# Starting addresses of the expert layers' split activations in SBUF, 16 and 48 bytes past a multiple of 256

## The chip, the cores and the metric

The kernel runs on one core of a Trainium2 chip. The metric is the device time of one launch in microseconds (us), as the median of several runs. Three runs of the kernel before gave 1542.0, 1543.3 and 1543.79 us. Engines are named as in the profile: PE is TensorE (its weight loads are shown apart as PEld), DVE is VectorE, ACT is ScalarE, POOL is GpSimd, SP is SyncE, which issues the DMAs.

## What is computed

One transformer layer on x of shape [16, 512, 128] in float32: a state-space mixer with residual and layer norm, then a mixture of 12 experts with residual and layer norm. Only the second half touches the change. Cut to that:

```python
dw1, dw2, dw3 = (top3_softmax(x_addr @ U.T) for U in (U1, U2, U3))   # [tokens, 12]
h = sum over e of dw1[:, e] * (x @ W1[e].T)      # [tokens, 512]
h = gelu(h)
y = sum over e of dw2[:, e] * (h @ W2[e].T)      # [tokens, 128]
y = y + dw3 @ b2
```

All 12 experts are computed densely for every token. The mixer also has one product of this kind that matters here, `silu(z) @ Wzg`.

## The kernel before, in words

The 16 sequences are 16 batches of 512 tokens. The program is one long straight list of instructions for each engine, written out by hand in Python: `body` is called once for each batch and lays, between the mixer steps of batch b, the expert steps of batch b-1, so that PE always has an expert product to work on while other engines prepare mixer operands. Semaphores order the engines; there is no scheduler, and SBUF tensors are placed one behind the other in the order in which `sb(...)` names them, each start rounded up to 32 bytes.

Large products are made in a split form. A float32 value is written as a high half (rounded to the type fp32r) and a low half (the rest, also fp32r), and `mm3` (lines 240 to 250) multiplies with three matmuls, each over 512 moving columns: high by high (L247), high by low (L248), low by high (L249):

```python
nc.tensor.matmul(ps, s_hi, m_hi, ...)         # L247: stationary s_hi, moving m_hi
nc.tensor.matmul(ps, s_hi, m_lo, ...)         # L248
last = nc.tensor.matmul(ps, s_lo, m_hi, ...)  # L249
```

Every one of these loads its own stationary operand of 128 columns first (a LDWEIGHTS on PEld). A row of the profile names the moving operand first and the stationary one second: `exp_bank<-sp_hi,w_hi` has `sp_hi` moving.

The split activations live in two tensors, `sp_hi` and `sp_lo`, each [128, 4, 512] in fp32r (line 144), so 8192 bytes in each partition. They are used in three places:

- `expert_in` (first expert layer): for each expert and each of 4 hidden slices of 128, one `mm3` with the weights `w1_hi`, `w1_lo` stationary and one quarter of `sp_hi`, `sp_lo` moving. 48 times three matmuls in a batch, except that expert 0 of the last batch reads `xT_hi`, `xT_lo`.
- `expert_out` (second expert layer): for each of 4 token blocks, 3 column groups and 4 slices, one `mm3` with a 128-column block of `sp_hi`, `sp_lo` stationary and `w2_hi`, `w2_lo` moving. 48 times three in a batch.
- `mix_zg`: 8 times three in a batch, `wzg_hi`, `wzg_lo` stationary and `sp_hi`, `sp_lo` moving.

They are written by casts on ACT (L1186, L641) or DVE (L1236) for the high half, and by a subtraction on POOL (L1190, L644, L1242) or DVE (L1239) for the low half, each of 128 partitions by 512 elements in most cases.

Line 103 puts an otherwise unused tensor `before_lines` of 128 bytes ahead of the weights. With it, the tensors `w1_hi` to `w2_lo`, `wbc`, `wz`, `wx`, `wzg`, `xT_hi`, `xT_lo`, `fbuf`, `acc` and also `sp_hi` (byte 209920) and `sp_lo` (byte 218112) all start at a multiple of 256 bytes, and so does every slice of them that a matmul of 512 columns reads. After `sp_lo` come only small tensors (`ix`, `ssum`, `dw2`, `dwpad`, `nrm`, `delta`, `a_rows`, `a_hi`, `a_lo`, `wbdt`, `router` and others), whose starts lie anywhere in steps of 32 bytes: `router` at 32 past a multiple of 256, `a_hi` at 96, `a_lo` and `a_rows` at 224, `dwpad` at 128.

Of the kernel before, what the change touches and what calls it, by code (L numbers as in the profile page):

```python
# [8 lines left out]
F32R = mybir.dt.float32r  # L9
# [6 lines left out]
P = 128  # L16
D = 128
NB, T = 16, 512
# [8 lines left out]
NH = HID // P  # L27
# [58 lines left out]
def layer_program(nc, x, Wz, Win, Wzg, Wout, dt_bias, A_log, D_param, P_w, U1T, U2T, U3T, W1T, W2T, b2, out):  # L86
    ctx = ExitStack()
    with ctx:
        def sb(name, shape, dt=F32):
            return ctx.enter_context(nc.sbuf_tensor(name, shape, dt))  # L90
# [50 lines left out]
        acc = sb("acc", [P, NC, D])  # L141
        acc_odd = sb("acc_odd", [P, D])
        wide = [fbuf[:, 2, :], fbuf[:, 3, :]]
        sp_hi, sp_lo = sb("sp_hi", [P, NH, T], F32R), sb("sp_lo", [P, NH, T], F32R)
        lg = fbuf[:, 3, 0:NC * NR * E].rearrange("p (g e) -> p g e", e=E)
        mx = fbuf[:, 3, NC * NR * E:NC * NR * (E + 8)].rearrange("p (g e) -> p g e", e=8)
        ix = sb("ix", [P, NC * NR, 8], U32)
# [1655 lines left out]
```

How the kernel before makes its waits and increments, by code:

```python
        def wait(eng, name, b, k=None):  # L213
            p = prods[name]
            v = (b.off - p.start) * p.n * p.step + ((p.n if k is None else k) - p.less) * p.step
            seen = waited.setdefault(id(eng), {})
            if (b.reg is None and v <= 0) or seen.get(name, -10**9) >= v:
                return
            seen[name] = v
            eng.wait_ge(p.sem, v if b.reg is None else b.reg * (p.n * p.step) + v)
            if eng is SP:
                alone(SP)
# [75 lines left out]
        def round_rest(n, src, hi, lo):  # L299
            DVE.tensor_copy(hi, src).then_inc(sems["chain"], 1)
            DVE.wait_ge(sems["chain"], n)
            DVE.tensor_tensor(lo, src, hi.bitcast(F32), ALU.subtract).then_inc(sems["cast"], 1)
# [1 line left out]
        def setup(eng):  # L305
# [3 lines left out]
                SP.dma_start(st_wz, Wz[:, :]).then_inc(sems["wz"], 16)  # L309
                SP.dma_start(bias_b[:, :], dt_bias.partition_broadcast(P)).then_inc(sems["decay_par"], 16)
                SP.dma_start(neg_a[:, :], A_log.partition_broadcast(P)).then_inc(sems["decay_par"], 16)
                SP.dma_start(d_b[:, :], D_param.partition_broadcast(P)).then_inc(sems["decay_par"], 16)
                SP.dma_start(st_wzg, Wzg.rearrange("(k p) n -> p k n", p=P)).then_inc(sems["wzg"], 16)
                SP.wait_ge(sems["pad"], 5)
                SP.dma_start(dA_dram.rearrange("h (c t) -> (h c) t", t=P), cum_t[0:H * NC, :]).then_inc(sems["zero"], 16)
                SP.dma_start(pw, P_w[:, :]).then_inc(sems["small"], 16)
```

## Time and profile before

| what | value |
|---|---|
| median of three runs | 1543.3 us (1542.0 to 1543.79) |
| the profiled execution's own time | 1542.65 us |
| its span, first to last instruction | 1540.9 us |
| mean granted TensorE clock | 0.998 of full speed |
| PE busy | 1525.7 us, 99% of the span, 8646 matmuls |
| DVE, ACT, POOL busy | 1115.0, 598.1, 658.3 us |
| DMA | 73 GB/s over the span |

The busy time of an engine is the time in which at least one of its instructions was under way. Matmuls overlap: the next one starts before the one ahead has ended, so the mean duration of a matmul (some 390 ns) is not what it costs. What it costs is the distance from its start to the next one's start, which is read from the timeline. The chain of waits tells which engine's work the end of the program follows from.

### The profile page before, as it was taken

How to read it: one execution, taken by the hardware profiler on the slowest of the kernel's cores; microseconds unless marked ns; L12 is line 12 of the kernel's file. 1: busy time of each engine (PE TensorE's matmuls, PEld its weight loads, DVE VectorE, ACT ScalarE, POOL GpSimd, SP SyncE). 2: the span in 40 equal slices, each digit the busy share in tenths (PEclk: the TensorE clock that was granted, in tenths of full speed). 3: DMA queues.
4: the chain of work that ended last, by engine and by line, in shares of the span. 5: the costliest groups of instructions: out<-in, count | busy, mean ns of one | idle time of the engine just before them, and what ended most of it. 6: DMA issues, size and time to landing. Idle time of an engine off the chain costs nothing.

```text
span 1540.9 us, 25335 instructions
## 1 busy us (share of the span) xinstructions
PE 1525.7 (99%) x8646; PEld 1250.4 (81%) x8646; DVE 1115.0 (72%) x3113; ACT 598.1 (39%) x1360; POOL 658.3 (43%) x751
## 2 busy tenths in 40 slices
PE   9999999999999999999999999999999999999998
PEld 7778888888888888888788888888888888887886
DVE  7677776877768687686776768777686776767755
ACT  6643424425244351533525244242443515335130
POOL 6671623616145270643616336162451705436040
PEclk9999999999999999999999999999999999999999
DMA  6340312314023140321403123040230403214020
GB/s 180 100 148 29 118 42 67 100 29 135 18 77 90 30 137 15 103 71 46 120 11 125 45 61 106 28 132 21 72 95 29 138 15 96 76 39 128 14 78 7
DMA packets 81456, 114.53 MB, mean 74 GB/s; under 512 B 10144, under 2 KB 37296, under 8 KB 81328
## 3 DMA queue, kind: packets, MB, share of 16 engines
q1 hardware_dynamic: 81328, 112.92, 24.6%
q8 instruction: 68, 1.11, 0.3%
q14 instruction: 60, 0.49, 0.1%
HBM read 107.76 MB, written 5.13 MB: 73 GB/s over the span
## 4 chain that ended last, share of the span: by engine, by line
PE 93%; POOL 3%; DVE 1%; issue 1%; DMA 1%; SPq 0%; ACT 0%; POOLq 0%; DVEq 0%
PE exp_bank L247 23%; PE exp_bank L249 22%; PE exp_bank L248 22%; PE mix_bank L896 4%; PE mix_bank L922 3%; PE mix_bank L247 3%; PE mix_bank L249 3%; PE mix_bank L904 3%; PE mix_bank L248 3%; PE mix_bank L793 1%; PE turn_bank L1249 1%; PE mix_bank L525 1%; PE mix_bank L739 1%; PE mix_bank L1013 1%; POOL Wt L856 1%
## 5 line engine op out<-in xcount | busy, mean ns | idle before, releaser
L1190 POOL TENSOR_TENSOR sp_lo<-fbuf,sp_hi 128x512 fp32r<-128x512 f32 (+2 forms) x201 | 243.4, 1214 | 176.9 <-ACT sp_hi L1186 106.9
L247 PE MATMUL exp_bank<-w_hi,sp_hi 128*128 128x512 f32 x768 | 304.0, 396 | 0.8 <-POOL sp_lo L1242 0.8
L247 PE MATMUL exp_bank<-sp_hi,w_hi 128*128 128x512 f32 x764 | 303.5, 397 | 0.1
L249 PE MATMUL exp_bank<-w_hi,sp_lo 128*128 128x512 f32 x768 | 299.7, 390 | 0.0
L248 PE MATMUL exp_bank<-w_lo,sp_hi 128*128 128x512 f32 x768 | 298.9, 389 | 0.0
L249 PE MATMUL exp_bank<-sp_hi,w_lo 128*128 128x512 f32 x764 | 298.3, 391 | 0.0
L248 PE MATMUL exp_bank<-sp_lo,w_hi 128*128 128x512 f32 x764 | 297.8, 390 | 0.0
L1289 DVE SCALAR_TENSOR_TENSOR acc<-exp_bank,dw,acc 128x128 f32<-128x128 f32 x384 | 132.4, 345 | 137.2 <-PE exp_bank L249 136.6
L1186 ACT CAST sp_hi<-fbuf 128x512 fp32r<-128x512 f32 (+2 forms) x203 | 120.0, 592 | 272.5 <-DVE fbuf L1156 216.5
L856 POOL TENSOR_TENSOR Wt<-Wt,Gh 128x512 f32<-128x512 f32 x128 | 184.8, 1445 | 21.0 <-DVE Wt L848 21.0
L247 PEld LDWEIGHTS exp_bank<-sp_hi,w_hi 128*128 128x128 f32 x764 | 143.7, 188 | 38.2 <-issue 8.9
L559 POOL TENSOR_TENSOR delta<-delta,bias_b 128x32 f32<-128x32 f32 x16 | 4.1, 256 | 388.4 <-ACT delta L535 383.7
L249 PEld LDWEIGHTS exp_bank<-w_hi,sp_lo 128*128 128x128 f32 x768 | 144.1, 188 | 31.1
L247 PEld LDWEIGHTS exp_bank<-w_hi,sp_hi 128*128 128x128 f32 x768 | 144.2, 188 | 30.8 <-POOL sp_lo L1242 1.3
L822 ACT ACTIVATE Gh<-Gm,delta 128x128 f32<-128x128 f32 x512 | 163.7, 391 | 13.2 <-POOL Wt L856 13.2
L249 PEld LDWEIGHTS exp_bank<-sp_hi,w_lo 128*128 128x128 f32 x764 | 143.7, 188 | 31.0
L248 PEld LDWEIGHTS exp_bank<-w_lo,sp_hi 128*128 128x128 f32 x768 | 144.4, 188 | 28.8
L248 PEld LDWEIGHTS exp_bank<-sp_lo,w_hi 128*128 128x128 f32 x764 | 143.8, 188 | 28.7
L848 DVE TENSOR_TENSOR_SCAN Wt<-seg_b,unit_bank 128x512 f32<-128x512 f32 x124 | 149.5, 1207 | 22.7 <-PE mix_bank L904 19.7
L1156 DVE TENSOR_TENSOR fbuf<-turn_bank,row_b 128x512 f32<-128x512 f32 x189 | 126.8, 675 | 11.4 <-DMA row_b<-dw_rows 11.1
L1289 DVE SCALAR_TENSOR_TENSOR acc_odd<-exp_bank,dw,acc_odd 128x128 f32<-128x128 f32 x320 | 109.4, 342 | 0.0
L1242 POOL TENSOR_TENSOR sp_lo<-fbuf,sp_hi 128x512 fp32r<-128x512 f32 x30 | 40.0, 1332 | 135.2 <-DVE sp_hi L1236 135.2
(267 smaller groups left out, 2286.1 us busy)
## 6 DMA issues: line engine op xcount, KB each, us to landing
row_b<-dw_rows SPq DMA_DIRECT2D x189, 256.0 KB, 3.3
seg_b<-dA_rows SPq DMA_DIRECT2D x124, 256.0 KB, 3.5
ctd<-cum_rows SPq DMA_DIRECT2D x128, 96.0 KB, 3.2
x_in<-in_x SPq DMA_DIRECT2D x16, 256.0 KB, 2.8
result<-acc SPq DMA_DIRECT2D x15, 256.0 KB, 2.2
fbuf<-in_W1T SPq DMA_DIRECT2D x12, 256.0 KB, 3.5
acc<-in_W2T SPq DMA_DIRECT2D x5, 256.0 KB, 3.5
x_in<-in_W2T SPq DMA_DIRECT2D x5, 256.0 KB, 2.8
```

Source lines behind the costliest of these rows:

```text
L247: nc.tensor.matmul(ps, s_hi, m_hi, start=start and j == 0, stop=False, skip_group_check=onto)
L248: nc.tensor.matmul(ps, s_hi, m_lo, start=False, stop=False, skip_group_check=onto)
L249: last = nc.tensor.matmul(ps, s_lo, m_hi, start=False, stop=stop and j == n - 1, skip_group_check=onto)
L822: last = AC.activation(G[:, c, :], Gm[:, c, :], ACT.Copy, scale=delta[:, c, h:h + 1])
L848: sig("scan", DVE.tensor_tensor_scan(W, first_seg[h % 4] if first(b) else seg_b[h % 2][:, :], unit[:, :], 0.0, ALU.mult, ALU.add))
L856: sig("W", PO.tensor_tensor(W, W, Gh[h % 2][:, :, :].rearrange("p c t -> p (c t)"), ALU.mult))
L896: PE.matmul(ps[j * HD:(j + 1) * HD, tok(c)], Xd[:, c, h * HD:(h + 1) * HD], Wt[:, q % 2, at:at + P], start=(c == 0 and not first(b)), stop ...
L904: last = PE.matmul(ps[j * HD:(j + 1) * HD, tok(c)], S[n, c - 1, q * HD:(q + 1) * HD], ctd[n, q % 2, (c - 1) * P:c * P], start=False, stop= ...
L1156: sig("xw", DVE.tensor_tensor(wide[e % 2], rb[:, :], row_b[e % 2][:, :], ALU.mult))
L1186: sig("xw_hi", AC.copy(hi[:, cols], wide[e % 2][:, cols]))
L1190: sig("xw_lo", on.tensor_tensor(lo[:, cols], wide[e % 2][:, cols], hi[:, cols].bitcast(F32), ALU.subtract))
L1289: sig("comb", DVE.scalar_tensor_tensor(dst, ps, w, dst, ALU.mult, ALU.add))
```

## The change

The two tensors of split activations get 16 bytes of padding at either end, and the program uses the part between. Nothing else is edited; each engine has the same instructions in the same order, with the same shapes and waits.

```diff
-        sp_hi, sp_lo = sb("sp_hi", [P, NH, T], F32R), sb("sp_lo", [P, NH, T], F32R)
+        LINE = 4
+        sp_hi, sp_lo = (sb(n, [P, NH * T + 2 * LINE], F32R)[:, LINE:LINE + NH * T].rearrange("p (k t) -> p k t", k=NH)
+                        for n in ("sp_hi", "sp_lo"))
```

The padded `sp_hi` is 8224 bytes long and still begins at byte 209920, so its used part begins at 209936, 16 past a multiple of 256. The padded `sp_lo` begins at 218144 and its used part at 218160, 48 past a multiple of 256. A quarter of either is 2048 bytes and a block of 128 columns is 512 bytes, so every slice that a matmul, a cast or a subtraction touches has the same 16 or 48. The small tensors behind them all move up by 64 bytes, so `router` is now 96 past a multiple of 256, `a_hi` 160, `a_rows` and `a_lo` 32 and `dwpad` 192. Lines behind the edit have numbers that are higher by 2.

## Rows read from the trace of the kernel before

**Rows 1.** The page: busy time, the granted clock in 40 slices, the chain that ended last
```profile
PE 1525.7 (99%) x8646; PEld 1250.4 (81%) x8646; DVE 1115.0 (72%) x3113; ACT 598.1 (39%) x1360; POOL 658.3 (43%) x751
...
PEclk9999999999999999999999999999999999999999
...
PE 93%; POOL 3%; DVE 1%; issue 1%; DMA 1%; SPq 0%; ACT 0%; POOLq 0%; DVEq 0%
```
**Rows 2.** Waits of PE over the whole span: us in total, times, longest
```profile
PE mix_bank L896 <- POOL Wt L856: 2.4, 1, 2.4
PE turn_bank L1464 <- POOL ident L325: 2.2, 1, 2.2
PE exp_bank L247 <- POOL sp_lo L1242: 0.8, 1, 0.8
```
**Rows 3.** Busy time in two batches of the steady part, with matmul counts and clock
```profile
core 0: us, PE busy (x) PEld busy (x) DVE busy (x) ACT busy (x) POOL busy (x), PEclk, DMA share, GB/s
585.68:679.43 93.75, 93.75 (x531) 76.91 (x531) 68.70 (x195) 36.22 (x83) 39.60 (x45) 1.00 0.24 72
679.43:773.16 93.73, 93.73 (x531) 76.91 (x531) 68.71 (x195) 36.20 (x83) 39.58 (x45) 1.00 0.24 71
```
**Rows 4.** Groups of matmuls on sp_hi and sp_lo: xcount, busy us, mean ns
```profile
L249 PE MATMUL exp_bank<-w_hi,sp_lo 128*128 128x512 f32 x768 | 299.7, 390 | 0.0
L248 PE MATMUL exp_bank<-sp_lo,w_hi 128*128 128x512 f32 x764 | 297.8, 390 | 0.0
L247 PE MATMUL mix_bank<-sp_hi,wzg_hi 128*128 128x512 f32 x120 | 46.8, 390 | 0.2 <-ACT fbuf L1080 0.2
L247 PE MATMUL exp_bank<-sp_hi,wzg_hi 128*128 128x512 f32 x8 | 3.2, 401 | 0.0
```
**Rows 5.** Timeline of PE, steady stretch of 512-column matmuls: start us, us, instruction
```profile
632.03 0.39 PE L249 MATMUL exp_bank<-sp_hi,w_lo 128*128 128x512 f32 x1
632.25 0.39 PE L247 MATMUL mix_bank<-wx_hi,xT_hi 128*128 128x512 f32 x1
...
641.55 0.39 PE L249 MATMUL exp_bank<-sp_hi,w_lo 128*128 128x512 f32 x1
```
**Rows 6.** The same timeline just ahead, behind short matmuls
```profile
628.93 0.27 PE L678 MATMUL mix_bank<-ident,a_rows 128*32 128x128 f32 x1
628.96 0.26 PE L752 MATMUL mix_bank<-a_hi,strict_r 128*128 128x24 f32 x1
629.07 0.26 PE L752 MATMUL mix_bank<-a_lo,strict_r 128*128 128x24 f32 x1
629.18 0.39 PE L754 MATMUL mix_bank<-a_rows,upper 128*128 128x32 f32 x2
629.40 0.47 PE L247 MATMUL exp_bank<-sp_hi,w_hi 128*128 128x512 f32 x1
629.72 0.39 PE L248 MATMUL exp_bank<-sp_lo,w_hi 128*128 128x512 f32 x1
629.95 0.40 PE L249 MATMUL exp_bank<-sp_hi,w_lo 128*128 128x512 f32 x1
630.18 0.40 PE L247 MATMUL exp_bank<-sp_hi,w_hi 128*128 128x512 f32 x1
630.42 0.39 PE L248 MATMUL exp_bank<-sp_lo,w_hi 128*128 128x512 f32 x1
630.64 0.39 PE L249 MATMUL exp_bank<-sp_hi,w_lo 128*128 128x512 f32 x1
```
**Rows 7.** The chain of waits in order of time: a stretch of 32 short matmuls
```profile
679.43 3.58 PE mix_bank L922 x32
```
**Rows 8.** Durations of the instructions that write the split halves, min/median/max
```profile
L1186 ACT CAST sp_hi<-fbuf x203: 297/621/627, 74.2 to 1489.2; 128x512 fp32r<-128x512 f32 x88, 128x384 fp32r<-128x384 f32 x7, 128x128 fp32r<-128x128 f32 x7
L1190 POOL TENSOR_TENSOR sp_lo<-fbuf,sp_hi x201: 456/1291/1593, 79.5 to 1490.2; 128x512 fp32r<-128x512 f32 x87, 128x384 fp32r<-128x384 f32 x7, 128x128 fp32r<-128x128 f32 x7
L1242 POOL TENSOR_TENSOR sp_lo<-zg,sp_hi x2: 1282/1332/1383, 1499.2 to 1501.9; 128x512 fp32r<-128x512 f32 x2
```

## Prediction

> **What bounds the kernel now.** I read the page first. PE is busy for 1525.7 of 1540.9 us, every slice shows a full granted clock (2.4 GHz), and the chain that ended last is 93% PE [rows 1]. Then the waits of PE: the longest entry is 2.4 us, once, and the only one on a tensor of this change is 0.8 us, once, on `sp_lo` in the last batch [rows 2]. Then two batches of the steady part side by side: both take 93.7 us, PE is busy for all of it with 531 matmuls, and the two agree to 0.02 us [rows 3]. So for the time only one thing counts: how far apart PE's matmuls start. What ACT, DVE and POOL do is hidden, until one of them makes PE wait.
>
> The distance of starts is read from the timeline. From the matmul at 632.03 to the one at 641.55 there are 42 steps in 9.52 us, or **226.7 ns a step** [rows 5]. That stretch holds matmuls with `sp_hi` or `sp_lo` moving and others with `wx` and `xT` only, and all step alike. 512 columns at 2.4 GHz are 213.3 ns, so each step has 13.4 ns on top, while the next 128 stationary columns are read from SBUF beside the 512 moving ones. Every operand in that stretch starts at a multiple of 256 bytes. Behind short matmuls the pace is worse for a while: from 629.72 to 632.03 there are ten steps in 2.31 us, 231.0 ns each, with 0.22 us as the shortest (630.42 to 630.64) and 0.47 us for two as the longest (629.95 to 630.42) [rows 5, 6]. So the step isn't a constant of 512 columns; something of a few nanoseconds in it varies, then settles.
>
> **How many matmuls the change reaches.** With `sp_hi` or `sp_lo` as an operand: three groups of 768 in the second expert layer, three of 764 in the first, three of 120 + 8 in `mix_zg` (one row of each kind stands in [rows 4]). Together 2304 + 2292 + 384 = 4980. At 226.7 ns they fill 1129 us of the span. One nanosecond a step is worth 4.98 us, and what a measurement of this kernel can tell from no change, 0.2% or 3.1 us, is 0.62 ns a step.
>
> **The change, part by part.**
>
> 1. *Reads of the moving operand from 16 or 48 instead of 0* (first layer and `mix_zg`, 2676 matmuls). The trace has no 512-column matmul off a multiple of 256. The nearest rows are short ones: moving `a_hi` (96 past), `a_lo` and `a_rows` (224 past) start 0.11 us apart [rows 6], as do the 32 short ones on aligned `wout` and `zg`, 3.58 / 32 = 0.112 us [rows 7]. So an odd start costs nothing that two digits show, but these read 24 to 32 columns and are paced by the load of 128 stationary columns, so the cover would hide a few nanoseconds. Price taken: 0.
> 2. *Loads of the stationary operand from 16 or 48* (second layer, 2304). The weight load runs beside the matmul ahead, and PEld is busy for 76.91 of 93.75 us [rows 3], so a load that was one column longer stays hidden. Price taken: 0.
> 3. *The two reads against each other.* This is what can't be excluded. Bounds from both sides: at best the whole 13.4 ns go, 4980 x 13.4 = 67 us, so 1543 - 67 = 1476; at worst each step is like the slowest pair, 235 ns, 4980 x 8.3 = +41 us, so 1584. The steady row is the nearest to both ends, because it shows steps untouched by all else that reads and writes SBUF meanwhile: DVE busy 68.70, POOL 39.60 and DMA a quarter of the time in a batch, and still one pace [rows 3, 5]. A read path that let those streams pass unfelt is not likely to care which 16 bytes an operand starts with. Price taken: 0.
> 4. *Writes of the halves to 16 and 48* by ACT, POOL and DVE. The medians are 621 and 1291 ns [rows 8]. If each became a tenth longer (0.06 and 0.13 us), PE, which waits for `sp_lo` once in the program [rows 2], would feel it at that one place, below 0.3 us with both subtractions of the last batch [rows 8]. Cover: every half is made well ahead of its product. Price 0 to +0.3 us.
> 5. *The small tensors moved by 64 bytes.* Moves of 64 keep their starts at odd places, where they were already. Price 0.
>
> The sum: 0 + 0 + 0 + 0.3 at most. The profiled execution took 1542.65 us (its span and 1.75 around it), 0.65 below the median of the runs. I forecast the median unchanged, **1543.3 us**.
>
> **A rule on each side.** Steps off a multiple of 256 but on a multiple of 16 are seen at 0.11 us like the others [rows 6, 7]. By that rule, the trace agrees: the Trainium skill, SBUF — State Buffer, Specifications (TRN2), says that SBUF is read in lines of 16 bytes, and 16 and 48 both keep every operand on a line, by which the sum is 0. Against that stands the 226.7 ns, which the same skill would not give: TensorE: Matmul & The Clock Gate, section "Wait — 56ns, not 53.3ns?", has N columns at 2.4 GHz plus about 2.5 ns, which I work out as an estimate of 215.8 ns for 512. No row here shows that pace.
>
> **The rivals.**
>
> *A. No change* (1540 to 1546): as above.
>
> *B. Faster: the stationary and the moving stream collide because both start at the same place in SBUF.* For it: 13.4 ns that the columns don't explain are paid at each step; a load of 128 columns is 32 pieces of 16 bytes, and 13.4 ns are 32 cycles at 2.4 GHz, one for each piece; and the settling behind short matmuls looks like two streams finding a phase. Shifting one of them by an odd number of 16-byte pieces would end it. Against it: the moving stream passes about two columns (512 in 213.3 ns) for each one of the load (128 in at most 112 ns, the step of short matmuls that each load 128 [rows 7]), so their relation sweeps through all phases within one matmul whatever the start. Prices: if steps go to the shortest one seen, 0.22 us, 4980 x 6.7 = 33 us, 1510; if five sixths of the 13.4 go, 55 us, 1488; all of it 1476. A step with nothing on top is seen nowhere in this trace, so I leave the last sixth out.
>
> *C. Slower: the pace doesn't settle, or an operand that starts inside a larger block costs one more fetch.* Place: all 4980. If they step as behind short matmuls, 231.0 ns, that is 4980 x 4.3 = +21 us, **1565**; one extra cycle at 1.2 GHz (0.83 ns) would be +4 us, 1547. It decides from 0.62 ns a step. For it: all operands of the steady 226.7 are aligned, and nothing shows that they need not be; the ten slower steps show that this path can run slower for more than 2 us. Against it: the short matmuls off alignment. At the slowest pair's pace it would be 1584.
>
> *D. Slower through an engine off PE*: writes at odd starts grow so much that PE waits. It takes more than the idle time ahead of those engines; POOL is busy 39.60 of 93.75 us [rows 3]. Below 1546 if at all.
>
> **How the numbers follow.** A 0.42 (with D's harmless part); B 0.30, of it 0.14 near 1510 and 0.16 near or below 1488; C 0.26, of it 0.19 up to 1566 and 0.07 beyond; D 0.02. Hence faster 0.30, same 0.42, slower 0.28. The likeliest case has a range of its own of 1540 to 1546. Since cases of both signs hold most of the chance, the range reaches to five sixths of the excess below (1488) and to the unsettled pace above (1566), and leaves out some 0.1 to 0.15: the last part of B and the worst of C.
>
> **What the changed profile would show.** A: 42 steps in 9.52 us in the stretch behind `mix_ends`, 93.7 us a batch. B or C: the steps of matmuls on `sp_hi`/`sp_lo` away from 226.7 ns, while those in the same stretch with `wx` and `xT` alone, which the change doesn't touch, stay at it; a steady batch has 144 + 144 + 24 = 312 steps of the first kind, so its 93.7 us move by 0.31 us for each nanosecond. If the two layers differ, it is the moving or the stationary read alone. D: new rows in PE's waits on `sp_hi` or `sp_lo`. The prediction is wrong if the batch moves by more than 0.2 us.

## The result, and the profile after

The changed kernel takes 1563.03 us (median of four runs, 1561.27 to 1563.69); the kernel before, on the same chip, 1542.78 us. The ratio is 1.0128 with a 95% interval from 1.0116 to 1.014: **slower by 20 us**. The forecast was no change; the time lies in the stated range, two us below what rival C gave (1565).

The page of the changed kernel, lines that answer to [rows 1]:

```profile
PE 1545.3 (99%) x8646; PEld 1252.5 (80%) x8646; DVE 1110.8 (71%) x3113; ACT 598.2 (38%) x1360; POOL 658.5 (42%) x751
...
PEclk9999999999999999999999999999999999999999
...
PE 92%; POOL 3%; DVE 1%; issue 1%; DMA 1%; SPq 0%; ACT 0%; POOLq 0%; DVEq 0%; ACTq 0%
```

The span grew from 1540.9 to 1561.2 us, and PE's busy time by 19.6 us with it, at the same granted clock. ACT and POOL are busy as long as before. The waits of PE, against [rows 2]:

```profile
PE turn_bank L1466 <- POOL ident L327: 2.2, 1, 2.2
PE mix_bank L898 <- POOL Wt L858: 2.2, 1, 2.2
PE exp_bank L249 <- POOL sp_lo L1244: 0.8, 1, 0.8
```

No wait has grown. Busy time in two batches of the steady part, against [rows 3]:

```profile
core 0: us, PE busy (x) PEld busy (x) DVE busy (x) ACT busy (x) POOL busy (x), PEclk, DMA share, GB/s
592.53:687.54 95.01, 95.01 (x532) 77.09 (x531) 68.60 (x195) 36.20 (x83) 39.67 (x45) 1.00 0.24 71
687.54:782.56 95.02, 95.02 (x532) 77.09 (x531) 68.58 (x195) 36.20 (x83) 39.61 (x45) 1.00 0.25 70
```

A batch takes 95.02 us where it took 93.74, 1.28 more, and 16 batches of that are 20.5 us, against 20.3 by which the span grew: the whole loss. The same matmuls simply start farther apart. The timeline of PE in the stretch of [rows 5] (start us, us, instruction):

```profile
639.64 0.39 PE L251 MATMUL exp_bank<-sp_hi,w_lo 128*128 128x512 f32 x1
639.87 0.40 PE L249 MATMUL mix_bank<-wx_hi,xT_hi 128*128 128x512 f32 x1
640.10 0.40 PE L250 MATMUL mix_bank<-wx_lo,xT_hi 128*128 128x512 f32 x1
640.34 0.40 PE L251 MATMUL mix_bank<-wx_hi,xT_lo 128*128 128x512 f32 x1
640.57 0.39 PE L249 MATMUL mix_bank<-sp_hi,wzg_hi 128*128 128x512 f32 x1
...
649.35 0.39 PE L251 MATMUL exp_bank<-sp_hi,w_lo 128*128 128x512 f32 x1
```

The same 42 steps take 9.71 us instead of 9.52: 231.2 ns a step instead of 226.7. The three matmuls on `wx` and `xT`, whose operands stand where they stood, take 0.70 us (639.87 to 640.57), so they too step more than 230 ns each. In the second expert layer it is slower still:

```profile
608.71 0.39 PE L251 MATMUL exp_bank<-w_hi,sp_lo 128*128 128x512 f32 x1
...
610.81 0.39 PE L251 MATMUL exp_bank<-w_hi,sp_lo 128*128 128x512 f32 x1
...
612.91 0.40 PE L251 MATMUL exp_bank<-w_hi,sp_lo 128*128 128x512 f32 x1
```

18 steps in 4.20 us are 233.3 ns each, in the settled part of a stretch, and each half of them takes 2.10 us. In the kernel before, the pace of 231 ns lasted for ten steps behind short matmuls [rows 6] and then fell to 226.7. Now a stretch of the second layer stays at 233.3, and one of the first at 230 to 231.

These are settled paces too, only slower ones. The trace holds the starts to the nanosecond, finer than the views print them. In the kernel before, the steps of a settled stretch are 226, 227, 227, over and over. In the changed kernel those of the second layer are 236, 233, 231, over and over: an unbroken stretch of 36 matmuls of that layer ends at 226.7 ns a step in all 45 cases before, and at 233.3 in all 45 cases after.

### The profile page after: what moved, and what is told of

The parts are those of the page before. It is cut to its first block, busy times and chain, and to the rows that moved or that the text cites. A ratio compares the mean times of both kernels' runs of the same rounds, so it can differ in the third digit from the quotient of the medians.

```text
span 1561.2 us, 25335 instructions
## 1 busy us (share of the span) xinstructions
PE 1545.3 (99%) x8646; PEld 1252.5 (80%) x8646; DVE 1110.8 (71%) x3113; ACT 598.2 (38%) x1360; POOL 658.5 (42%) x751
## 4 chain that ended last, share of the span: by engine, by line
PE 92%; POOL 3%; DVE 1%; issue 1%; DMA 1%; SPq 0%; ACT 0%; POOLq 0%; DVEq 0%; ACTq 0%
PE exp_bank L249 23%; PE exp_bank L250 22%; PE exp_bank L251 22%; PE mix_bank L898 4%; PE mix_bank L924 3%; PE mix_bank L249 3%; PE mix_bank L251 3%; PE mix_bank L250 3%; PE mix_bank L906 3%; PE mix_bank L795 1%; PE turn_bank L1251 1%; POOL w_lo L447 1%; PE mix_bank L741 1%; PE mix_bank L1015 1%; PE mix_bank L527 1%
## 5 line engine op out<-in xcount | busy, mean ns | idle before, releaser
L249 PE MATMUL exp_bank<-w_hi,sp_hi 128*128 128x512 f32 x768 | 308.1, 401 | 0.8 <-POOL sp_lo L1244 0.8
L250 PE MATMUL exp_bank<-w_lo,sp_hi 128*128 128x512 f32 x768 | 304.3, 396 | 0.0
```

Of the source, the lines that this page charges most:

```text
L249: nc.tensor.matmul(ps, s_hi, m_hi, start=start and j == 0, stop=False, skip_group_check=onto)
L250: nc.tensor.matmul(ps, s_hi, m_lo, start=False, stop=False, skip_group_check=onto)
```

## The experiments

All are edits of the kernel before. A time of one execution is given; where runs were repeated, the median and the interval. The kernel before gave 1542.0 to 1544.4 us beside them. The finest measure is the length of a batch, read from the chain of waits as the distance between two neighbouring stretches of 32 matmuls on `wout` and `zg`; in the kernel before it is 93.7 us [rows 3, 7]. "Place" is the start modulo 256 bytes.

**Which part of the change, and how far.** Four kernels. `small64` leaves the halves alone and moves the small tensors:

```diff
         sp_hi, sp_lo = sb("sp_hi", [P, NH, T], F32R), sb("sp_lo", [P, NH, T], F32R)
+        sb("behind", [P, 16])
```

> The two split halves stay at multiples of 256; only the small tensors behind them move up by 64 bytes, as in the change. Theory of the two streams (the step of a 512-column matmul depends on how far the start of the moving operand and the start of the stationary operand lie apart in SBUF, modulo some small power of two) and theory of the block (an operand that starts inside a larger block costs one more fetch): both expect no change, 93.74 us a batch and about 1543 us, since the large operands don't move. Theory of the small tensors (a read or write of one of them at its new place is slow): 95.0 us a batch and 1563 us.

`both16`, `both32` and `both64` put both halves into one tensor of 16448 bytes that starts at a multiple of 256, at the place n (4, 8 or 16 elements), with the small tensors moved as in the change:

```diff
-        sp_hi, sp_lo = sb("sp_hi", [P, NH, T], F32R), sb("sp_lo", [P, NH, T], F32R)
+        halves = sb("sp_halves", [P, 4112], F32R)
+        sp_hi = halves[:, n:n + NH * T].rearrange("p (k t) -> p k t", k=NH)
+        sp_lo = halves[:, NH * T + n:n + 2 * NH * T].rearrange("p (k t) -> p k t", k=NH)
```

> Both halves at 16 past a multiple of 64, weights at multiples, small tensors as in the change. Two streams: slower as the change, since moving and stationary start 16 bytes apart, 94.5 to 95.2 us a batch and 1555 to 1566 us. Block larger than 16 bytes: the same 95.0 us a batch. A third theory, that the difference between high and low half (32 bytes) is what costs, as the moving operand changes from one to the other within each group of three: no change, 93.74 us.

> Both halves at 32 past a multiple of 64. Two streams: if the period is 32 bytes, 93.74 us a batch; if it is 64 or more, another pace than 226.7 ns, either way, 93 to 95.5 us a batch. Block: 93.74 us if the block is 32 bytes, 95.0 us (1563) if it is 64 or more.

> Both halves at 64 past a multiple of 256. Two streams: no change if the period is 64 bytes or less (93.74 us a batch, 1543 us). Block: no change for a block of 64 bytes or less, 95.0 us a batch for one of 128 or 256.

Measured: `small64` 1542.98 us; `both16` 1559.62; `both32` 1569.4; `both64` 1562.89. The chain of `small64` and of `both32`:

```profile
585.49 3.58 PE mix_bank L923 x32
679.25 3.58 PE mix_bank L923 x32
```

```profile
593.90 3.58 PE mix_bank L924 x32
689.40 3.58 PE mix_bank L924 x32
```

93.76 and 95.50 us a batch. The small tensors cost nothing. A difference between high and low half isn't needed (`both16` has none). Any block or period of 64 bytes or less is ruled out by `both64`.

**One place for all, or a certain place?** `all32` makes the unused tensor ahead of the weights 160 bytes long, `all128` leaves it out, and `halves128` leaves it out and puts the halves back to a multiple of 256:

```diff
-        sb("before_lines", [P, 32])
+        sb("before_lines", [P, 40])      # all32; in all128 and halves128 the line is left out
```

> Every SBUF tensor, weights and halves alike, starts 32 bytes higher than in the kernel before, so nothing is at a multiple of 256 but moving and stationary operands keep their distance of 0. Theory of the relation (the step depends on how far the two operands that are read at once lie apart): no change, 93.74 us a batch, 1543 us. Theory of the absolute place (a start at other than 0 modulo 256 costs by itself): as with both halves at 32 or more, 95.5 us a batch and 1569 us.

> The unused 128 bytes ahead of the weights are left out, so all large tensors start 128 past a multiple of 256, with distance 0 between the two operands. Relation: 1543 us. Absolute place: slower, unless its period is 128 bytes or less; but halves at 64 were slow, so it would be 128 at least.

> Weights and the mixer's operands at 128 past a multiple of 256, halves at a multiple of 256: distance 128. Relation with a period of 128 bytes: 1543 us, 93.74 us a batch. Relation with a period of 256 or more: another pace than 226.7 ns, 94.8 to 95.5 us a batch. Absolute place: mixer-only products slow too.

Measured: `all32` 1543.41 us, `all128` 1542.91, `halves128` 1567.49. The chain of `all32` and of `halves128`:

```profile
585.96 3.58 PE mix_bank L922 x32
679.71 3.58 PE mix_bank L922 x32
```

```profile
593.53 3.58 PE mix_bank L923 x32
688.93 3.58 PE mix_bank L923 x32
```

93.75 and 95.40 us. So no operand has to be at a multiple of anything larger than 32 bytes for the fast pace; what counts is that the operands start at the same place. A distance of 128 costs nearly as much as one of 32 (24 and 27 us against the kernel before beside each). In the kernel before, `w1_hi` starts at byte 16640 and `sp_hi` at 209920, which differ by 256 modulo 512, and that costs nothing. So the period isn't 128 bytes or less, and it isn't 512 or more; 256 is the power of two that is left.

**One half alone, and less than 16 bytes.** `hi16_only` has the high half at 16 and the low one at 0; `lo48_only` the low one at 48 and the high one at 0; `both8` has both at 8.

> Only the high half is at 16, the low half stays at a multiple of 256. If each read of a half at an odd distance costs for itself, two of the three matmuls of a group are touched and the loss is about two thirds of that with both at 16 (two thirds of 17.6 us: 1554). If the pace is a matter of the whole sequence settling or not, one operand of three is enough to keep it from settling: 1556 to 1566 us, the whole loss or more.

> Only the low half is moved, to 48; the high half is at a multiple of 256. Simultaneous load: in the first layer one moving operand of three is at distance 48 (the middle one), in the second the load of the low half meets the middle matmul. Slower by some third to the whole of the change's 20 us: 1550 to 1563 us. If only high halves mattered: 1543 us.

> Both halves at 8 bytes past a multiple of 256, inside a piece of 16. If only the distance in whole pieces of 16 bytes counts, and a moving stream of 2048 bytes that touches one piece more costs nothing by itself: 1543 us. If any distance counts: 1552 to 1566 us.

Measured: 1558.28, 1571.14 and 1562.53 us. `lo48_only` lies above all that its expectation allowed (1550 to 1563). So there is no share for each moved operand: with one half moved, it loses 28 us, more than the change does with both. And pieces of 16 bytes play no part that shows: 8 bytes cost 20 us.

**A pace that depends on how a stretch began.** The timeline of `both16` holds the clearest rows of the study. Two stretches of the second expert layer in one batch, the same instructions on operands at the same places modulo 256:

```profile
603.53 0.39 PE L251 MATMUL exp_bank<-w_hi,sp_halves 128*128 128x512 f32 x1
603.76 0.39 PE L249 MATMUL exp_bank<-w_hi,sp_halves 128*128 128x512 f32 x1
...
604.21 0.39 PE L251 MATMUL exp_bank<-w_hi,sp_halves 128*128 128x512 f32 x1
...
611.01 0.39 PE L251 MATMUL exp_bank<-w_hi,sp_halves 128*128 128x512 f32 x1
611.24 0.97 PE L1015 MATMUL mix_bank<-router,fbuf 128*128 128x36 f32 x8
612.05 0.64 PE L506 MATMUL mix_bank<-ident,x_in 128*128 128x128 f32 x4
...
612.75 0.40 PE L250 MATMUL exp_bank<-w_lo,sp_halves 128*128 128x512 f32 x1
...
620.69 0.40 PE L251 MATMUL exp_bank<-w_hi,sp_halves 128*128 128x512 f32 x1
```

From 604.21 to 611.01 there are 30 steps of 226.7 ns; from 612.75 to 620.69 there are 34 of 233.5. One fell into the fast pace within its first few matmuls and kept it, the other never found it. What decides between them isn't shown. So the unequal place doesn't add a fixed price to a matmul; the same sequence can have more than one steady pace.

How often it takes which can be counted over the 45 unbroken stretches of 36 matmuls of the second layer in each trace, by their last twelve steps. In `both16` 12 of them end at 226.7 ns and 33 at 233.3, in `hi16_only` 15 end at 226.7, and in the other slow kernels, those further down included, none does. The stretches of 60 matmuls of the first layer have one pace for each kernel, one to three of some 30 aside: 228.9 ns in `both64`, 230.0 in the change, 231.7 in `both16`, 233.3 in `both32`, 235.6 in `lo48_only`. So with unequal places the steps do settle, nearly always on a slower pace, and which one depends on the distances. In the kernel before, `small64`, `all32`, `all128` and `own_aligned` it is 226.7 in both layers.

**Which distance counts?** My theory now was that a moving stream and the weight load that runs at the same time (that of the next matmul) must start at one place. `low_all64` lets all high tensors (weights, mixer operands, halves) start at 0 and, behind 64 unused bytes, all low ones at 64, so that each of the three matmuls of a group meets the load of the next at distance 0:

```diff
         sb("before_lines", [P, 32])
+        w1_hi = sb("w1_hi", [P, E, HID], F32R)
...
+        sp_hi = sb("sp_hi", [P, NH, T], F32R)
+        sb("between", [P, 16])
+        w1_lo = sb("w1_lo", [P, E, HID], F32R)
...
+        sp_lo = sb("sp_lo", [P, NH, T], F32R)
```

> All low tensors (weights, mixer operands and halves) start at 64 past a multiple of 256, all high ones at 0. In the order high-high, high-low, low-high each moving operand then meets a weight load (that of the next matmul) at distance 0: high with high, low with low, high with high. But the second and the third matmul have a stationary operand of their own at distance 64, and successive moving operands lie 64 apart. Theory that the distance counts between the moving stream and the weight load that runs at the same time: no change, 1543 us, 93.74 us a batch. Theory that it counts between a matmul's own two operands, or between successive moving operands: slower, as with both halves at 64, 1555 to 1563 us.

`low_all64_order` has the same places and another order in `mm3`:

```diff
-                nc.tensor.matmul(ps, s_hi, m_hi, ...)
                 nc.tensor.matmul(ps, s_hi, m_lo, ...)
+                nc.tensor.matmul(ps, s_hi, m_hi, ...)
                 last = nc.tensor.matmul(ps, s_lo, m_hi, ...)
```

> The same places as low_all64, but the first two matmuls of each group change places (high-low, high-high, low-high). Now the low moving operand meets the load of a high one and the next high moving operand the load of a low one: distance 64 in two of three. Theory of the simultaneous load: slower, 1555 to 1565 us, with not one address changed. Theory that only a matmul's own operands or the addresses as such count: as low_all64.

Measured: `low_all64` 1561.46 us, ratio 1.0121 (1.0104 to 1.0138); `low_all64_order` 1562.95. Their chains:

```profile
592.32 3.58 PE mix_bank L931 x32
687.24 3.58 PE mix_bank L931 x32
```

```profile
593.10 3.58 PE mix_bank L931 x32
688.09 3.58 PE mix_bank L931 x32
```

94.92 and 94.99 us a batch. **The theory of the simultaneous load fell**: with that distance at 0 everywhere the loss is nearly the same as with it at 64 in two of three. Left were a matmul's own two operands, or all operands that follow each other. `own_distance0` keeps the places of `low_all64` and multiplies high by high, high by high and low by low, so that each matmul's own operands start at one place; `own_aligned` is the same edit of `mm3` at the old places. Both leave the cross terms out and count the high product twice.

```diff
-                nc.tensor.matmul(ps, s_hi, m_lo, ...)
-                last = nc.tensor.matmul(ps, s_lo, m_hi, ...)
+                nc.tensor.matmul(ps, s_hi, m_hi, ...)
+                last = nc.tensor.matmul(ps, s_lo, m_lo, ...)
```

> Places as in low_all64, but each group of three multiplies high by high, high by high and low by low (so the cross terms are left out and the high product counts double). Every matmul's own two operands are then at distance 0, while successive moving operands (high to low and back) and the loads beside them are at 64 in two of three. Theory of a matmul's own two operands: 1543 us, 93.74 us a batch, steps of 226.7 ns. Theory of the sequence (the pace settles only if all operands that follow each other start at the same place modulo 256): slower, 1555 to 1565 us, 94.6 to 95.2 us a batch.

> Control for own_distance0: the same three products (cross terms left out, high product twice), with all places as in the kernel before. Both theories: 1543 us, 93.74 us a batch. Another time would mean that the products themselves change the pace.

Measured: 1565.4 us and 1542.33 us; the control shows that the products themselves don't matter. The chain of `own_distance0`:

```profile
592.83 3.58 PE mix_bank L931 x32
688.08 3.58 PE mix_bank L931 x32
```

95.25 us a batch. So the theory of the own operands fell too, and the theory of the sequence stands: operands that follow each other must start at one place. It is a rule and not a cause. No single relation explains the runs: `low_all64` is slow with each moving operand at the place of the load beside it, `own_distance0` with each at the place of its own stationary operand, and the first layer of `both16` with all moving operands at one place. The runs don't tell how much each relation contributes where several are unequal.

`mixer64` tests the rule in another way. It orders the tensors so that the expert weights, `wzg` and the halves are at 0 and `wbc`, `wz`, `wx` and `xT` at 64, again behind 64 unused bytes.

> The mixer's own split operands (wbc, wz, wx and xT, high and low) start at 64 past a multiple of 256, the halves and the weights they meet at 0. Each group of three has all its operands at one place, but the program passes from one place to the other some eight times a batch. Own operands: 1543 us. Sequence: each passage unsettles the pace for some ten steps at 231 ns, 8 x 10 x 4.3 ns = 0.35 us a batch, 94.1 us a batch and about 1548 us, with both kinds of stretch back at 226.7 ns in between.

Measured: 1543.85 us, and its chain and timeline:

```profile
585.50 3.58 PE mix_bank L923 x32
679.38 3.58 PE mix_bank L923 x32
```

```profile
632.56 0.40 PE L250 MATMUL mix_bank<-wx_hi,xT_lo 128*128 128x512 f32 x1
...
634.42 0.39 PE L249 MATMUL mix_bank<-sp_lo,wzg_hi 128*128 128x512 f32 x1
634.64 0.39 PE L250 MATMUL mix_bank<-sp_hi,wzg_lo 128*128 128x512 f32 x1
...
638.27 0.39 PE L248 MATMUL mix_bank<-wx_hi,xT_hi 128*128 128x512 f32 x1
```

From 632.56, the last matmul on the mixer's operands, to 634.42 there are eight steps of 232.5 ns; from 634.64 to 638.27 sixteen of 226.9. This passage unsettles the pace for eight steps or so, and it settles again as soon as all that follows is at one place. The whole costs 0.14 us a batch, less than the 0.35 I had worked out from eight passages of ten steps each. The run's own time would fit the theory of the own operands as well; it is the disturbed steps at the passage that speak for the sequence. `mixer64` is a control for `low_all64` too: both move `wout`, `zg`, `fbuf` and the other tensors behind the gap by 64 bytes, and here that costs nothing that shows.

What stays open is the mechanism inside the chip. The runs show that the pace depends on how the starts of moving and stationary operands lie to each other, with a period of 256 bytes, and that a disturbance lasts over several matmuls. They don't show which buffer or arbiter does it, nor what the 13.4 ns above 213.3 are: no run was faster than 226.7 ns in a settled stretch. Places with distances of 80, 96 or 112 bytes weren't tried, nor was any version found that beats both kernels.

## Why the prediction was wrong

**What bounds the kernel** was right. PE bounds it, its few waits are as they were, and the loss lies wholly in the distance of matmul starts. The price of a nanosecond, 4.98 us, counts only the touched steps; by it the loss of 20.3 us would be 4.1 ns each. In fact the untouched ones carry a part: those on `wx` and `xT` step more than 230 ns where they stand in threes between the others.

**Parts 1 and 2** (reads from another place cost nothing by themselves) were right, but for operands that all moved alike, which I hadn't considered: `all32` and `all128` show it. I took as evidence the short matmuls on `a_hi` and `a_rows`. Those rows answered for a single read at an odd place, not for a sequence.

**Part 3** is the step that failed: it put the two reads against each other at nothing, and they cost the whole +20.3 us. I priced them at 0, because the steady rows showed PE's pace untouched by DVE, POOL and DMA [rows 3, 5]. That indifference is real, and the engines' writes at the new places were harmless too, but it says nothing on PE's own two reads. What the runs showed in its place: with moving and stationary operands at different places modulo 256 bytes, steps settle at 230 to 231 ns in the first layer and at 233.3 in the second, where they settled at 226.7. I had put the effect between -67 and +41 us. One row in hand bore on it: the ten steps of 231.0 ns behind short matmuls [rows 5, 6] show that the pace isn't given by the columns alone but is found by settling. All places in the trace being equal, no row of 512 columns told what unequal ones would do, so the price of 0 had none behind it either.

**Part 4 and rival D**: part 4 was right and D didn't occur, PE's waits are as they were. **Part 5**: right, `small64` agrees to 0.02 us a batch.

**Rival B** (equal starts collide, unequal ones would be faster) is the wrong way round: equal starts are the fast case wherever they were run (`small64`, `all32`, `all128`, `own_aligned`). **Rival C** was right in sign and, but for the untouched steps that slowed too, in place. That its 1565 came within two us is luck: it took the average of the ramp, 231.0 ns, for all touched steps, while the settled paces are 230 to 231 and 233.3, and the same cause cost between 14 and 28 us at other distances. Its first mechanism, a pace that doesn't settle, was close but not what happened: it settles on a slower one. Its second one, a larger block that costs one more fetch, fell with `all32`, which starts 32 bytes into every such block and loses nothing.

**The rules.** The Trainium skill, SBUF — State Buffer, Specifications (TRN2), gives lines of 16 bytes; I drew from it that starts at multiples of 16 are all alike. The runs don't agree with that use of it: 16, 32, 64 and 128 bytes of distance cost 18 to 27 us. The same page of the Trainium skill, section "Who interferes with whom", says that PE's two read ports, for moving operand and LDWEIGHTS, are independent. `halves128` (+24 us) and `both16` (+18 us) show a pace that depends on how the places of the two operands lie to each other; so for the pace the two reads can't be taken as independent, and the measurement decides. The estimate of 215.8 ns, from the Trainium skill's page TensorE: Matmul & The Clock Gate, section "Wait — 56ns, not 53.3ns?", was the settled pace of no run.

**Signs I named**: "those with `wx` and `xT` alone stay at 226.7" was wrong, and it was wrong for the reason that matters, since the pace belongs to the sequence and not to the instruction. Where six matmuls on the mixer's operands follow each other in the changed kernel, the trace has 236, 228, 233, 231, 226, 227 ns: the pace comes back to 226.7 only at the fifth. "If the two layers differ, it is the moving or the stationary read alone" misled too: the layers differ (230 to 231 and 233.3 ns), yet neither read is slow by itself, as `all32` shows.

## What to carry to other kernels

Where PE streams split matmuls back to back, let all their large operands, moving and stationary, high and low, start at the same place modulo 256 bytes; which place didn't matter here (0, 32 and 128 were run). An innocent resize of any tensor ahead of them can break that, so pin it, and after any change of layout read the distance of starts in a long stretch of equal matmuls: here 226.7 ns against 229 to 236 is 1 to 2% of the kernel with not one instruction changed. A row that shows a pace settling over several steps is a warning that it can also settle elsewhere.

## What the runs showed that I had not expected

- Matmuls of the second layer on operands at the same places modulo 256 run at 226.7 or at 233.5 ns a step within one batch of `both16`, and keep that pace to the end of the stretch.
- The loss isn't additive: low half alone at 48 costs 28 us, high half alone at 16 costs 14 us (each against the kernel before beside it), and both together, in the change, 20 us.
- 8 bytes of distance cost 20 us, and 128 bytes 24 us; 256 bytes cost nothing.
